# Weight-quantization loads split between the SyncE and GpSimd queues in an 8-core attention and FFN kernel

## The reference

```python
# x: (8, 2048, 1024); 16 heads of 64; 8 groups of 128 channels
x = _layernorm(x + attn(x, w_qkv, w_proj, b_proj))
x = _layernorm(x + ffn(x, w_gate, w_up, w_down))

def _weight_quant(w):                      # one scale for a whole matrix
    scale = 1.0 / jnp.clip(jnp.mean(jnp.abs(w)), 1e-05)
    return jnp.clip(jnp.round(w * scale), -1.0, 1.0) / scale
def _act_quant(x):                         # one scale for each row
    scale = 127.0 / jnp.clip(jnp.max(jnp.abs(x), -1, keepdims=True), 1e-05)
    return jnp.clip(jnp.round(x * scale), -128.0, 127.0) / scale
# ffn: bitlinear(silu(bitlinear(x, w_gate)) * bitlinear(x, w_up), w_down)
```

## Time and profile before

| | us |
|---|---|
| median of 3 runs | 2130.78 |
| the three runs | 2126.21, 2130.78, 2167.39 |
| the profiled execution | 2124.53 |
| its span on the slowest core (first to last instruction) | 2121.8 |
| spans of its eight cores | 2108.9 to 2121.8 |
| TensorE / VectorE / ScalarE busy, share of the span | 63% / 44% / 45% |
| DMA, mean over the span | 148 GB/s |

### The profile page before, as it was taken

How to read it: one execution, slowest core, us unless ns; L and a number is a source line. 1 busy time by engine, 2 the same in 40 slices (tenths; PEclk the granted TensorE clock), 3 DMA queues, 4 the chain that set the end, 5 groups by cost and what they waited for, 6 DMA issues and landing times.

```text
span 2121.8 us, 20608 instructions; the slowest of 8 cores (2108.9 to 2121.8 us)
## 1 busy us (share of the span) xinstructions
PE 1346.3 (63%) x5502; PEld 463.1 (22%) x5502; DVE 924.0 (44%) x1742; ACT 948.4 (45%) x1079; POOL 44.6 (2%) x84
## 2 busy tenths in 40 slices
PE   0057667576747763067663899845999647676582
PEld 0011111111111110011111344412444213222230
DVE  1138840544566433583618444444444440303023
ACT  2267888488838883068860212254121460101011
POOL 0000000000000000000000000000000000000000
PEclk9999888688868886578775899977999869899896
DMA  6779950135742777826704433333444426676762
GB/s 187 224 247 330 319 179 1 41 100 163 206 117 84 219 217 215 228 99 178 229 7 118 104 78 75 75 112 99 88 96 95 117 87 173 160 197 187 184 204 79
DMA packets 371458, 314.02 MB, mean 148 GB/s; under 512 B 296593, under 2 KB 298641, under 8 KB 369298
## 3 DMA queue, kind: packets, MB, share of 16 engines
q1 hardware_dynamic: 339712, 234.97, 42.6%
q10 hardware_dynamic: 23186, 48.38, 6.7%
q0 software_dynamic: 8448, 29.37, 3.8%
HBM read 161.49 MB, written 83.89 MB: 116 GB/s over the span
## 4 chain that ended last, share of the span: by engine, by line
PE 43%; ACT 14%; DMA 13%; DVE 12%; SPq 8%; issue 7%; ACTq 2%; DVEq 1%; POOL 0%; POOLq 0%
PE ps L84 43%; ACT A L84 14%; DVE A L84 8%; SPq L84 8%; DMA A<-wg 2%; DMA wdt_sb<-wdqT_s 2%; DVE ln_sb L84 2%; ACTq L84 2%; DMA wtstage<-wdq_s 2%; DMA A<-wqkv 2%; DMA xre_f<-xp_s 1%; DVE h L84 1%; DMA wdqT_s<-wtstage 1%; DMA A<-wu 1%; DMA xbf_s<-A 1%
## 5 line engine op out<-in xcount | busy, mean ns | idle before, releaser
L84 ACT ACTIVATE A<-ps,cst_sb 128x1024 bf16<-128x1024 f32 (+1 forms) x544 | 552.7, 1105 | 246.4 <-DVE A L84 157.9
L84 PE MATMUL ps<-A,A 64*128 64x512 bf16 (+1 forms) x2048 | 529.6, 432 | 204.9 <-ACT A L84 179.6
L84 PE MATMUL ps<-wg_sl,xqT 128*128 128x512 bf16 x1024 | 265.7, 406 | 114.9 <-DVE h L84 101.8
L84 PE MATMUL ps<-wdt_sb,hqT 128*128 128x512 bf16 x1024 | 243.0, 397 | 111.0 <-DMA wdt_sb<-wdqT_s 52.7
L84 PEld LDWEIGHTS ps<-A,A 64*128 64x128 bf16 (+1 forms) x2048 | 125.6, 106 | 607.1 <-issue 603.9
L84 ACT ACTIVATE A<-ps,scg 128x512 f32<-128x512 f32 x128 | 88.0, 687 | 331.5 <-PE ps L84 309.5
L84 DVE SCALAR_TENSOR_TENSOR h<-ps,scu,A 128x512 bf16<-128x512 f32 x128 | 96.1, 751 | 216.6 <-ACT A L84 212.3
L84 DVE TENSOR_SCALAR A<-A,wsc 128x1024 f32<-128x1024 f32 x96 | 72.3, 753 | 203.5 <-DMA A<-wg 97.1
L84 PEld LDWEIGHTS ps<-wg_sl,xqT 128*128 128x128 bf16 x1024 | 103.9, 103 | 253.2 <-issue 146.7
L84 DVE TENSOR_SCALAR A<-A 128x1024 f32<-128x1024 f32 (+1 forms) x208 | 144.3, 694 | 34.1 <-DVE A L84 17.7
L84 PEld LDWEIGHTS ps<-wdt_sb,hqT 128*128 128x128 bf16 x1024 | 100.6, 101 | 253.5 <-issue 151.6
(11 more groups left out here) (66 smaller groups left out, 702.7 us busy)
## 6 DMA issues: line engine op xcount, KB each, us to landing
A<-wg SPq DMA_DIRECT2D x64, 512.0 KB, 5.7
A<-wu SPq DMA_DIRECT2D x64, 512.0 KB, 5.8
A<-wd SPq DMA_DIRECT2D x64, 512.0 KB, 6.0
wdt_sb<-wdqT_s SPq DMA_DIRECT2D x128, 256.0 KB, 3.4
hq_s<-h ACTq DMA_DIRECT2D x16, 1024.0 KB, 3.9
A<-x SPq DMA_DIRECT2D x16, 512.0 KB, 6.9
xt_s<-A POOLq DMA_DIRECT2D x16, 512.0 KB, 3.9
A<-xt_s ACTq DMA_DIRECT2D x16, 512.0 KB, 3.3
```

Of the source, the lines that this page charges most:

```text
L84: ins = getattr(eng, meth)(*args, **kw)
```

## The change

Every load of a unit is cut into two column halves. Columns 0 to 511 stay on SyncE's queue; columns 512 to 1023 are issued on GpSimd's queue, with the same wait on c_wq3 put into GpSimd's list, and with semaphores of their own (s_wqg0, s_wqg1), for which VectorE waits as well. Besides, two small loads at the start share one semaphore, and a debug semaphore is renamed (that code isn't built).

```diff
     dma("scalar", cst[:, :], cst_d[:, :], "s_cst")
-    n = dma("scalar", A12[0:1, 0:1024], bproj_d[:, :], "s_bp")
+    n = dma("scalar", A12[0:1, 0:1024], bproj_d[:, :], "s_cst")
...
-    wait("tensor", "s_bp", 16)
+    wait("tensor", "s_cst", 32)
...
         stg = A5[:, par * 1024:(par + 1) * 1024]
         if gidx >= 2:
             wait("sync", "c_wq3", 3 * (gidx - 1), future=True)
+            wait("gpsimd", "c_wq3", 3 * (gidx - 1), future=True)
         else:
             wait("sync", "c_wma", 96, future=True)
-        dma("sync", stg, tii, f"s_wqp{par}")
+            wait("gpsimd", "c_wma", 96, future=True)
+        dma("sync", stg[:, 0:512], tii[:, 0:512], f"s_wqp{par}")
+        dma("gpsimd", stg[:, 512:1024], tii[:, 512:1024], f"s_wqg{par}")
...
             wait("vector", f"s_wqp{par}", 16 * (gidx // 2 + 1))
+            wait("vector", f"s_wqg{par}", 16 * (gidx // 2 + 1))
...
-            wait("scalar", "s_cst", 16)
+            wait("scalar", "s_cst", 32)
```

More of the change, by code:

```diff
@@ L704, in build @@
             if debug and qc >= 1:
-                wait("scalar", "s_dbgA", c("s_dbgA"))
+                wait("scalar", "s_dbg", c("s_dbg"))
             arp = A8[:, p * 512:(p + 1) * 512]
@@ L737, in build @@
         if debug:
-            wait("vector", "s_dbgA", c("s_dbgA"))
+            wait("vector", "s_dbg", c("s_dbg"))
         em("vector", "reciprocal", A10[:, 64:128], A10[:, 0:64], inc=("c_rcp", 1))
@@ L742, in build @@
             wait("sync", "c_pve", c("c_pve"))
-            dma("sync", dbg_ar[:, :], A8[:, :], "s_dbgA")
+            dma("sync", dbg_ar[:, :], A8[:, :], "s_dbg")
         if attn_lvl < 3 and attn_lvl not in (6, 7):
@@ L793, in build @@
                 wait("sync", "c_radd", c("c_radd"))
-                dma("sync", dbg_rc[:, :], A10[:, :], "s_dbgA")
+                dma("sync", dbg_rc[:, :], A10[:, :], "s_dbg")
             if attn_lvl != 4:
@@ L839, in build @@
         wait("sync", "s_dbg", c("s_dbg"))
-        wait("sync", "s_dbgA", c("s_dbgA"))
+        wait("sync", "s_dbg", c("s_dbg"))
     def wu_slice_ap(par, ic):
```

## The result

The change made the kernel slower: 2184.97 us median of 9 runs (2170.43 to 2248.28) against 2127.23 us median of 10 runs of the kernel before (2118.12 to 2206.77). The ratio is 1.027, with a 95% interval of 1.0242 to 1.0297: +57 us, and not +16. Runs in which the cores of one die showed a lower clock and took over 1% longer than the others are left out of all ratios here.

The account below looks back on a forecast made before the run. The prediction took the third block's loop of weight loads and transposes as the bound. Six rounds x 2.85 = 17, less 1 at the block's head, gave +16 us: 2144 us, between 2140.5 and 2146.8, range 2118 to 2164.

Parts of the forecast that it names:

- the place: Third query block (qc = 2): TensorE and ScalarE stand still 70 us, waiting for the weight units; other blocks have cover.
- each microsecond on the loop is one of the kernel: Third block's rounds of 31.1 us: upwards without limit, downwards until the 70 us of standstill are used up.
- the halves save nothing: A 512 KB load has 1.3 us of transfer in 5.0; splitting leaves the fixed part, so no gain was counted.
- the small edits: The shared semaphore of two small loads at the start and the renamed debug semaphore, both costed at 0.
- Second: ... covered by the first wait, at 0.: Third block: the next group's second transpose waits for the late pending store; up to 3 us a round, counted as 0.
- my upper end of 6.2: Slowest assumed landing of the pending store after its issue, putting the second transpose's issue at 744.5; quickest 2.3 us.
- I take 0 for these loads: Loads where nothing stands in the halves' way: no change; ends -2.1 and +0.8 against the round's third term.
- the cover of 6.5: Second query block (qc = 1): VectorE finishes its 30 units 6.5 us before the row sums, so that much can be lost.
- The first wait: Round's head: GpSimd's first half load stands behind the third transpose's store, issued 3.15 us later; +2.85 us a round.
- the third term of the round: Second load of a round in the third block, issue to first pass: 6.29 us in one round, mean 5.6.
- The stated range: 2118 to 2164 us, from the lower case's middle to the upper ends on the median; 2 in 10 outside.
- each second half waiting for a whole unit on VectorE: Rival: GpSimd's half load issued only when a VectorE unit ends, 2.4 us late; +44 us, 2168 to 2175; chance 0.15.

Follow-up runs that it names:

- e1: The changed kernel with both halves of every load issued by SyncE and no waits for GpSimd; ratio 1.0013 to the kernel before.
- e7: The changed kernel with both halves issued by SyncE, but GpSimd's waits for the units left in its list; ratio 1.0069 to the kernel before.
- e2: The changed kernel with the pending store moved behind the second half load of the next group, not the sixth; ratio 1.0187 to the kernel before.
- e9: The changed kernel with SyncE's half of every load left out; executed once, 2133.04 us, where the kernel before took 2126.76.
- e3: The changed kernel with the first 32 units (w_down, second query block) loaded whole by SyncE; ratio 1.0228 to the kernel before.
- e8: The kernel before with w_down's 32 transposes moved into the first half of gate and up, 5 units a head pair in the third block; ratio 0.9768.
- e12: The kernel before with w_down's transposes in gate and up, two after each of sixteen slices, 5 units a head pair in the third block; 2069.16 us, ratio 0.9704.

## Why the prediction was wrong

What held: the place (nothing else moved), that each microsecond on the loop is one of the kernel, that the halves save nothing, that the small edits cost nothing (e1), that the second transpose waits for the pending store, and that the load at a round's head comes later. What failed, by its steps:

- **"Second: ... covered by the first wait, at 0."** This step carried the miss. It was worth +6.0 us a round, 29.8 in all. The wait was seen and its place was right; the cover was not there, for two reasons. First, the price. I let the second transpose land at 744.9, at most 3 us later, because before it lay behind a load on its own queue. The pending store lands 7.5 us after its issue (7.33 in the round shown), above my upper end of 6.2, and the transpose issued then still takes 4.4 us: it lands 12.1 us after the first transpose's issue where it was 6.7. Even by my own upper end, an issue at 744.5, it would have landed near 749. The last transpose is issued after 16.4 us where it was 10.1. Second, the logic. The half load that was to cover the delay stands behind the third transpose's store, and the third transpose stands behind the second on SyncE's queue (issued after 12.1 us, it was 8.8). So the cover is itself late by the same wait, and the two waits lie one behind the other. e7 and e2 separate it: with the waits alone the third block loses 9.3 us, and with the pending store moved forward 22 of its 45 come back. The difference between e7 and the changed kernel is GpSimd's queue: there the pending store lies behind a half load that is itself late, is issued 1.0 us later against the first transpose and takes 7.5 us and not 5.0. In e9, without SyncE's half, it takes 6.0.
- **"I take 0 for these loads"**, with an upper end of +0.8. Within a pair the last half lands at 0.5 + 5.4 = 5.9 us from the unit's end, against 5.1 before. In the second block fourteen pairs took 14.6 us more (from first to last first pass, 127.8 against 113.2), 1.04 a pair; the cover of 6.5 took its part, and 9.4 came through at the block's end (6.6 on the mean of the cores, where the loads took 12.6 more and the cover was 6.2). e3 gives nearly all of it back (604.9 at the block's end). I had put this block at 0 under its cover. The price per load was a size of about my upper end; it was the count that I didn't multiply: 14 x 0.8 = 11 was already over the cover.
- **The first wait**, +2.85 a round, measured +2.0. Nearly right in size, and by another way: SyncE's own half is late by the step above, so that GpSimd's is issued within about 1 us of it (771.66 and 771.68 in the round shown) and the 3.15 us never appear as such; what costs is that both halves land late there, SyncE's in 6.7 us and GpSimd's in 5.9 on the mean of the 40 rounds, where the whole took 5.1. In e2, where the late store is gone, the wait does appear: GpSimd's half is issued 2.2 us after SyncE's, and from the load to the first pass it is 8.5 us and not 5.3, +3.2. So this term was priced about right.
- **Smaller readings**: the third term of the round is 5.4 on the mean of its six loads (6.3, 5.5, 5.4, 5.1, 5.3, 4.9), not 5.6, and the second transpose landed at 744.3; neither changes the sum.
- **The stated range** ended at 2164, since I gave the upper ends of the terms only to the head and to the second load, and none to the term taken as covered.

The rival that came nearest in size, each second half waiting for a whole unit on VectorE (+44; the prediction calls it the second rival, in its list it is the third), is refuted as a mechanism. I sorted the half loads of GpSimd between 500 and 600 on all eight cores of the changed kernel by what VectorE does in the 1.2 us from their issue: 61 with VectorE busy for over 0.8 us of it land in 5.4 us (median), 99 with it busy for under 0.3 in 5.3. The 26 in between are left out. In e9 it is 3.8 and 3.9. What remains of the lock is the issue itself: 8 of those 61 took over 0.9 us, none of the 99. One of them, in GpSimd's timeline:

```profile
589.56 1.05 POOL L84 DMA_DIRECT2D A<-wd  x1 [5.82 <-DVE A L84]
```

and VectorE's first pass beside it:

```profile
589.74 0.75 DVE L84 TENSOR_SCALAR A<-A,wsc 128x1024 f32<-128x1024 f32 x1 [0.73 <-DMA A<-wd]
```

So the rule of the Trainium skill ("SBUF — State Buffer", section "SBUF: two separate sides") gave the right advice here, keep such loads off GpSimd's queue, and the trace agrees with its mechanism by half a microsecond in 8 of 61 cases; the loss has other causes. The Trainium skill also says, in "DMA: Bandwidth & Descriptors", section "Issuing engines are not separate DMA queues", that transfers of all issuing engines run on the same 16 engines, so that several issuers save only issue time. The trace agrees: with two issuers the last half lands 5.9 us after the unit's end, where the whole load of one issuer took 5.1.

Left open: why q1's packets go ahead of q0's when they were issued only half a microsecond before. The runs show that it is so and what it costs, not which part of the chip decides it.

## What to carry to other kernels

Before a transfer is moved to another engine's queue, write out that queue's list in order and follow everything that now stands behind the new wait: here it was one store that a transpose on the first queue waited for, and two transposes that had run together then ran one after the other. What is to cover a delay must not itself stand behind it. A term that is called covered needs an upper end like every other, and a price per piece has to be multiplied by the pieces before it is compared with the cover. And a loop made of latencies is helped by taking steps out of it (e8, e12), not by cutting its transfers.

## What the runs showed of the hardware that was not expected

- 256 KB loaded by GpSimd's queue alone land in 3.7 us, by SyncE's in 3.4. With both under way, issued 0.5 us apart, SyncE's is at 3.6 and GpSimd's at 5.4 (on all eight cores 3.9 and 3.4 alone, 5.3 and 3.8 together): the later queue bears most of the sharing.
- Cutting 96 loads of 512 KB into 192 of 256 KB on one queue changed the time by a factor of 1.0013 (0.9978 to 1.0049).
- GpSimd starts a transfer some 0.5 us after the semaphore that it waited for (0.48 in the chain of waits), SyncE 0.05 us after.
